# The shared network's down product of two token groups as three products of rounded words, with the experts' down weights loaded in two halves

## The reference, cut to what matters

```python
logits = x @ router_weight.T                 # 32 experts, top 4 of them per token
g = einsum('th,ehf->etf', x, w_gate); u = einsum('th,ehf->etf', x, w_up)      # F = 96
out = einsum('te,etf,efh->th', combine, silu(g) * u, w_down)
shared = silu(x @ sw_gate) * (x @ sw_up) @ sw_down                            # FS = 512
out = out + sigmoid(x @ sgate_w) * shared
```

## Time and profile before

| | us |
|---|---|
| median of 3 runs | 502.21 |
| lowest, highest | 502.06, 503.6 |
| the profiled execution | 502.63 |
| its span, first to last instruction | 500.5 |
| PE busy | 492.3 (98%) |
| DVE busy | 363.7 (73%) |
| ACT busy | 287.1 (57%) |
| POOL busy | 272.1 (54%) |

### The profile page before, as it was taken

One profiled execution on the slowest core, in us unless ns is written; L12 is line 12 of the kernel. 1 busy time (PEld: TensorE's weight loads), 2 busy tenths in 40 slices (PEclk: granted clock), 3 DMA queues, 4 the chain that ended last, 5 costly groups with the idle time before them and its releaser, 6 DMA issues.

```text
span 500.5 us, 13284 instructions
## 1 busy us (share of the span) xinstructions
PE 492.3 (98%) x3945; PEld 432.7 (86%) x3945; DVE 363.7 (73%) x1199; ACT 287.1 (57%) x719; POOL 272.1 (54%) x344
## 2 busy tenths in 40 slices
PE   7999999999999999999999999999999999999997
PEld 6999999999998888788888888888888888878886
DVE  5557888999886748834566777677767767379997
ACT  5777777877776635226477766677776662210110
POOL 2000477777777788881066767676676767500000
PEclk9999999999999999999999999999999999999999
DMA  6475577767745237934367666586766652399986
GB/s 212 136 224 184 172 255 222 220 222 214 219 165 179 101 110 181 250 132 108 91 186 229 202 197 195 174 238 182 217 197 194 183 188 101 96 402 377 327 361 208
DMA packets 65956, 100.77 MB, mean 201 GB/s; under 512 B 9856, under 2 KB 52864, under 8 KB 65792
## 3 DMA queue, kind: packets, MB, share of 16 engines
q1 hardware_dynamic: 48704, 60.30, 41.2%
q0 software_dynamic: 12672, 35.41, 19.5%
q10 hardware_dynamic: 4512, 4.23, 2.6%
HBM read 55.92 MB, written 43.97 MB: 200 GB/s over the span
## 4 chain that ended last, share of the span: by engine, by line
PE 90%; DVE 4%; DMA 2%; issue 1%; POOL 1%; ACT 1%; POOLq 0%; DVEq 0%; ACTq 0%; SPq 0%
PE bank L812 32%; PE bank L1108 14%; PE bank L1137 9%; PE bank L856 7%; PE bank L1104 5%; PE bank L1055 5%; PE bank L987 3%; PE bank L1018 3%; PE bank L1133 3%; PE bank L1004 3%; PE bank L1119 2%; PE bank L869 1%; PE bank L846 1%; POOL returned L515 1%; PE bank L972 1%
## 5 line engine op out<-in xcount | busy, mean ns | idle before, releaser
L484 POOL DMA_INDIRECT sent<-rows,slot x128 | 132.3, 1033 | 84.9 <-issue 83.6
L515 POOL DMA_INDIRECT returned<-arena,back x136 | 130.8, 962 | 77.1 <-DVE back L1638 35.6
L1108 PE MATMUL bank<-w_gu,arena 128*128 x416 | 79.7, 335 | 0.3 <-DVE resid L1278 0.3
L1108 PEld LDWEIGHTS bank<-w_gu,arena 128*128 128x128 f32 x416 | 66.3, 189 | 0.5 <-issue 0.5
L1606 DVE TENSOR_SCALAR arena<-bank,back_to 128x256 f32<-128x256 f32 x136 | 59.0, 475 | 3.0 <-issue 1.5
L542 ACT ACTIVATE act_t<-bank 128x512 f32<-128x512 f32 x24 | 14.4, 599 | 75.4 <-PE bank L812 75.4
L712 ACT COPY hnt<-w_gu 128x384 f32 x128 | 55.7, 511 | 0.0
L739 ACT ACTIVATE arena<-bank 128x192 f32<-128x192 f32 x68 | 22.4, 330 | 56.9 <-PE bank L1137 28.7
L1589 DVE TENSOR_TENSOR arena<-bank,arena 128x192 f32<-128x192 f32 x68 | 24.2, 356 | 41.6 <-ACT arena L739 40.2
L812 PE MATMUL bank<-w_hi_all,att_split 128*128 128x256 f32 x256 | 48.6, 292 | 0.0
L812 PE MATMUL bank<-hnt_rounded,ws_hi 128*128 128x512 f32 x160 | 48.4, 396 | 0.0
(11 more groups left out here) (216 smaller groups left out, 1057.3 us busy)
## 6 DMA issues: line engine op xcount, KB each, us to landing
arena<-returned SPq DMA_DIRECT2D x16, 1024.0 KB, 6.5
loaded<-sent SPq DMA_DIRECT2D x104, 134.0 KB
w_gu<-w_gate_up SPq DMA_DIRECT2D x32, 192.0 KB
sent<-rows SPq DMA_DIRECT2D x4, 1072.0 KB, 6.2
loaded<-sent SPq DMA_DIRECT2D x128, 33.5 KB
resid<-x SPq DMA_DIRECT2D x16, 256.0 KB, 3.7
att_plain<-ctx_t SPq DMA_DIRECT2D x16, 256.0 KB, 3.8
out<-resid ACTq DMA_DIRECT2D x7, 512.0 KB, 4.6
```

The lines of the kernel that those rows point to most:

```text
L484: pool.indirect_dma_start(out=sent, out_offset=bass.IndirectOffsetOnAxis(ap=slot[:, 2 * b + j, k:k + 1], axis=0), in_=rows[:, u, j, :], in ...
L515: pool.indirect_dma_start(out=returned, out_offset=bass.IndirectOffsetOnAxis(ap=back[:, t:t + 1], axis=0), in_=down_e[u][:, s, :], in_offs ...
L1108: last = pe.matmul(view[:, s, :], rows_t[:, s, c, :], w_gu[:, c, bass.ds(e[s], 1), :] .rearrange("p e f -> p (e f)"), start=(c == 0), stop ...
```

## The change

Four edits belong together.

1. The down products of groups 2 and 3 are made by `split_down`: `ws_d` and `act_t` are split into rounded words and rests, and 48 matmuls of float32r take the place of the 32 of float32. The order within a block f is: for each tile t hi by hi and hi by lo, then for each t lo by hi.
2. ACT rounds `ws_d` (`wd_hi`, 128x1024) behind group 2's first silu, and each block of `act_t` (`act_hi`, 128x512). DVE subtracts: `wd_lo` once (128x1024), ahead of group 2's third multiplication, and `act_lo` for each block (128x512), in the place of `act_t`.
3. `wd_hi`, `wd_lo` and `act_hi` lie in words 4096 to 8191 of `arena`, where the down weights of experts 16 to 31 come to lie. So SP loads only experts 0 to 15 where it loaded all, and the other 1.5 MB ahead of the tiles of pair 6, when `shared_psum` is 4.
4. TensorE's wait for `down_w` moves from ahead of step 0 to step 3, just ahead of the first `expert_down`, and waits for both loads; `copy_down` on ACT and DVE waits for both too.

```diff
@@ space @@
+        wd_hi, wd_lo = (plain_r[:, 4096 + FB * D * n:4096 + FB * D * (n + 1)].rearrange("p (f d) -> p f d", f=FB)
+                        for n in range(2))
+        act_hi = split[:, 0:FB * 512].rearrange("p (f t) -> p f t", f=FB)
         (w_plain,) = under(("w_plain", 4 * 512, F32))
+        (act_rounded,) = under(("act_rounded", FB * 512, F32R))
+        act_lo = act_rounded[:, :].rearrange("p (f t) -> p f t", f=FB)
         act_t = sb("act_t", [P, FB, 512])
...
+        def split_until(g, f):
+            return FB * (g - 2) + f + 1
@@ SP @@
-            sp.dma_start(w_dn, w_down).then_inc(S["down_w"], 16)
+            half = EXPERTS // 2
+            sp.dma_start(w_dn[:, 0:half, :], w_down[:, 0:half, :]).then_inc(S["down_w"], 16)
...
+                if pair == RING:
+                    wait(sp, "shared_psum", EARLY)
+                    sp.dma_start(w_dn[:, half:EXPERTS, :], w_down[:, half:EXPERTS, :]).then_inc(S["down_w"], 16)
                 wait(sp, "turned_psum", pair - RING + 1)
@@ ACT @@
+            def split_act_hi(g, f):
+                wait(act, "shared_act", FB * g + f + 1)
+                wait(act, "shared_psum", g if g > 2 else 0)
+                act.copy(act_hi[:, f, :], act_t[:, f, :]).then_inc(S["act_hi_ready"], 1)
+
             for g in range(2, EARLY):
                 for f in range(FB):
                     shared_silu(g, f)
+                    if g == 2 and f == 0:
+                        act.copy(wd_hi, ws_d[:, :, :]).then_inc(S["wd_hi_ready"], 1)
+                    if f > 0:
+                        split_act_hi(g, f - 1)
...
+                split_act_hi(g, FB - 1)
                 split_hn_hi(g + 1)
...
             def copy_down(pair, first):
                 if pair == FIRST_MIXED:
-                    act.wait_ge(S["down_w"], 16)
+                    act.wait_ge(S["down_w"], 32)
@@ PE @@
+            def split_down(g, behind={}):
+                wait(pe, "shared_added", GT * g)
+                if g == 2:
+                    pe.wait_ge(S["wd_lo_ready"], 1)
+                for f in range(FB):
+                    views = [sum_banks[t // 2][:, 256 * (t % 2):256 * (t % 2) + 256] for t in range(GT)]
+                    wait(pe, "act_hi_ready", split_until(g, f))
+                    for t in range(GT):
+                        pe.matmul(views[t], act_hi[:, f, P * t:P * t + P], wd_hi[:, f, :],
+                                  start=(f == 0 and t % 2 == 0), stop=False)
+                        pe.matmul(views[t], act_hi[:, f, P * t:P * t + P], wd_lo[:, f, :], start=False, stop=False)
+                    wait(pe, "act_lo_ready", split_until(g, f))
+                    for t in range(GT):
+                        last = pe.matmul(views[t], act_lo[:, f, P * t:P * t + P], wd_hi[:, f, :],
+                                         start=False, stop=(f == FB - 1 and t % 2 == 1))
+                    if f == FB - 1:
+                        last.then_inc(S["shared_psum"], 1)
+                    if f in behind:
+                        behind[f]()
...
-                shared_down(g, {2: first_transposes} if g == EARLY - 1 else {})
+                split_down(g, {2: first_transposes} if g == EARLY - 1 else {})
...
-            pe.wait_ge(S["down_w"], 16)
...
+                if pair == 3:
+                    pe.wait_ge(S["down_w"], 32)
                 if pair > 2:
                     expert_down(pair - 3, e[pair - 3])
@@ DVE @@
+            def split_act_lo(g, f):
+                wait(dve, "act_hi_ready", split_until(g, f))
+                dve.tensor_tensor(act_lo[:, f, :], act_t[:, f, :], act_hi[:, f, :].bitcast(F32), ALU.subtract) \
+                    .then_inc(S["act_lo_ready"], 1)
+
+            dve.wait_ge(S["wd_hi_ready"], 1)
+            dve.tensor_tensor(wd_lo, ws_d[:, :, :], wd_hi.bitcast(F32), ALU.subtract) \
+                .then_inc(S["wd_lo_ready"], 1)
             for g in range(2, EARLY):
                 for f in range(2 if g == 2 else 0, FB):
                     shared_mul(g, f)
+                    if g == 2 and f == 2:
+                        split_act_lo(g, 0)
+                    if f > 0:
+                        split_act_lo(g, f - 1)
+                split_act_lo(g, FB - 1)
                 split_hn_lo(g + 1)
...
             def copy_down(pair, first):
                 if pair == FIRST_MIXED:
-                    dve.wait_ge(S["down_w"], 16)
+                    dve.wait_ge(S["down_w"], 32)
```

More of the change, by code:

```diff
@@ L245, in build_xattn_moe @@
             "meant_ready", "meant_both_ready", "back_to_ready", "back_ready",
+            "wd_hi_ready", "wd_lo_ready", "act_hi_ready", "act_lo_ready",
             "sg_psum", "su_psum", "silu_ready", "shared_act", "shared_psum", "unit_psum", "shared_added",
```

## The result

The median of four runs is 511.5 us (510.13 to 511.7), against 502.24 us (502.06 to 503.6, four runs) for the kernel before on the same chip: a ratio of 1.0161, 95% interval 1.014 to 1.0182. The profiled execution took 510.13 us, with a span of 508.4 us against 500.5.

What follows compares the result with a forecast made beforehand. PE was taken as the bound, busy 98% of the span. Late weights 5.8, tiles 0.1 and clock 1.4 gave +7.3 us on 502.63, or 509.5 on the median, given as 509.2; range 504.8 to 511.8 us.

Steps and rivals of the forecast that it cites:

- the likeliest case: Second half lands late, PE idles 5.4 us before the first expert down product, clock falls; 509.2 us, chance 0.55.
- rival 4: Longer stall: sends held up 1.5 to 2 us, 10.8 us load, clock at half speed; 511.5 to 513 us, chance 0.15.
- the sum: Whole kernel: 5.8 us late weights, 0.1 tiles, 1.4 clock, +7.3 us on the profiled execution's 502.63.
- signs of being wrong: No PE idle time ahead of the first expert down product, or load issued before 242 us, would make the argument wrong.
- part 3: POOL's sends beside DVE's new subtractions: 0.7 us later (bounds 0 and 2), moving SP's whole list by as much.
- part 1 and 2: Down products of groups 2 and 3: matmuls gain 2.1 us, group 2's split waits leave 1.3 to 1.4 us.
- part 4: Second half of down weights: issued 243.0, 9.8 us to landing, PE waits 5.4 us; +5.8 us at first down product.
- rival 1: Second half lands sooner, at 248.6; PE waits about 2 us, clock stays; 503.7 to 505.7 us, chance 0.22.
- part 5: PE's clock after its idle wait: falls to 1.2 GHz, costing 1.4 us (bounds 0 and 2.7).
- the step: Load time of the second half: 1.57 MB at 213 GB/s, 7.4 us, plus 2.4 for start and end.
- Rivals 2 and 3: Weights in time, 1.4 us gained, 500.8 us (chance 0.04); or landing near 247 to 248.6, no change within 0.3% (0.04).
- Rival 5: Matmuls gain more or less than 1.4 us; lost at PE's wait, changes nothing while weights are late; no chance given.

Runs made afterwards that it cites:

- e1c: Changed kernel with the old float32 products and no splits, down weights still loaded in two halves: 510.43 us, ratio 1.0125 to the kernel before.
- e4c: Changed kernel with the wait for the second half of down weights moved from step 3 to step 8 on PE: 510.18 us, ratio 1.0126.
- e3c: Changed kernel with 24 unused matmuls ahead of PE's wait for the down weights: 509.39 us, ratio 1.0105 to the kernel before.
- e5: Changed kernel with the second half's load issued by ACT after group 3's down product, not by SP: 509.04 us, ratio 1.0113.
- e7c: Changed kernel with all down weights loaded at once as before, rounded words in attention's free spaces: 503.24 us, ratio 1.0004 to the kernel before.

## Why the prediction was right

The direction and the mechanism of the likeliest case held: the second half lands late, PE has one idle time of 5 to 6 us for it where there was none, and then works at the lower clock. The median lies 2.3 us above the forecast of 509.2, inside the whole range (504.8 to 511.8), but 0.5 us above that case's own range (507 to 511) and at the lower edge of rival 4. On the profiled execution the sum was 502.63 + 7.3 = 509.9, and 510.13 was measured. That this is so near is in part luck. PE's lateness at the first down product and behind it was forecast as 5.9 us, and is 4.9: the load was issued 1.7 us sooner, counted from the first load, and took 0.8 us longer. The clock was forecast as 1.4 us, and is 3.2. The earlier start of the whole profile then takes off 0.5 us.

One of the signs of being wrong did come: the load was issued at 240.83 us, before 242, and the last send ended 0.8 us earlier in place of up to 1 us later. The argument doesn't fall with it. In e1c and e4c the load was issued at 242.3 and 242.6 us, and PE waits as long, 5.5 and 5.7 us. The sign left no room for how much the sends vary (part 3 below).

**The products (part 1 and 2).** Gain 1.3 to 1.4 us at the end of group 3, by the two waits that stay in group 2. Measured: group 3 ends 1.4 us earlier from the common point. The subtraction for `wd_lo` on DVE, and what PE does at the start of group 2's down product:

```profile
211.22 1.16 DVE L1627 TENSOR_TENSOR att_rounded<-ws_d,att_rounded 128x1024 fp32r<-128x1024 f32 x1
```

```profile
212.49 0.36 PE L897 MATMUL bank<-att_rounded,att_split 128*128 128x256 f32 x1 [0.39 <-issue]
...
213.39 0.28 PE L899 MATMUL bank<-att_rounded,att_split 128*128 128x256 f32 x1
213.76 0.74 PE L902 MATMUL bank<-att_rounded,act_rounded 128*128 128x256 f32 x4
```

PE waits 0.39 us for `wd_lo` (forecast 0.4). From 213.39 to 213.76 are 0.37 us, where one product follows another in 0.12: some 0.25 us of wait for `act_lo` (forecast 0.3). The products themselves come every 0.12 us, as put down.

**The sends (part 3).** Forecast +0.7 us, measured -0.8 in the profiled execution. The mechanism is there, and smaller: in the stretch of the new subtractions two sends are long (timelines of POOL and DVE),

```profile
213.83 1.32 POOL L498 DMA_INDIRECT sent<-rows,slot  x1 [0.16 <-issue]
...
216.91 1.70 POOL L498 DMA_INDIRECT sent<-rows,slot  x1 [0.16 <-issue]
...
213.02 1.28 DVE L1623 TENSOR_TENSOR act_rounded<-act_t,att_split 128x512 fp32r<-128x512 f32 x2
...
216.54 1.22 DVE L1289 TENSOR_TENSOR hnt_rounded<-hnt,hn_hi 128x1024 fp32r<-128x1024 f32 x1 [0.26 <-ACT hn_hi L581]
```

where one of 1.61 was the earlier trace rows, which adds 0.4 us. The one of 1.70 stands beside the old subtraction (L1289, L1244 before), so that the new ones lengthen a single send, by 0.35 us. Both long sends start while a subtraction runs and end about one normal duration after it. A send that a subtraction joins later isn't lengthened: the one at 215.54 takes 0.97 us, though a subtraction starts 0.05 us behind it. What I hadn't seen is that the sends of attention, where the kernels are the same, differ from one trace to the next by more than that. Their time over 0.96 us a send, summed until 192 us, is 7.9 us in before, 7.7 in e1c, e3c and e4c, and 6.6 in after, e5 and e7c: two levels, some 1.1 us apart. In before this costs next to nothing, as POOL has 1% of the chain. Since the change hangs SP's load, and PE on it, on the last send, it now reaches the end. It fits that the other three runs of the kernel after took 511.4 to 511.7 us, 1.3 to 1.6 us more than the profiled one; that they are the executions with the slower sends is argued, not shown. Against these three the sum was 1.6 us low.

**The load (part 4).** Issue forecast for 243.0, measured 240.83: 1.5 us of it by the sends, 0.5 by the earlier start. Duration forecast 9.8 us with bounds of 6.3 and 10.8, measured 10.56 with tile loads in the same queue (9.2 for the first half, without them). By the DMA queue's records the last packet of 16 KB moves at 249.0 to 249.3 us, 8.4 us after the issue, where the step had 7.4, and the load counts as landed only 2.2 us behind it, while tile loads already fill the DMA engines (the step had 2.4 for start and end). So the step's rate was near, and rival 1, by which the half lands in 6.3 us, is refuted by every run: no half took less than 9.2. The estimate worked out from the Trainium skill ("SBUF — State Buffer", the section on the DMA setup-cost knee) was 5.6 us for the half; the measurement decides against it. Wait forecast 5.4 us, measured 5.9. The wait of 1.7 us for pair 4's tiles, which I had ahead of it, isn't in the profiled execution, where SP came earlier, but it is there in e3c (1.5) and e4c (1.7), where SP issued the load 49.8 and 50.0 us after the first one (forecast 50.1, measured in after 48.5). It changes nothing, since PE only loses there what it would lose later.

**The clock (part 5).** Forecast 1.4 us, between 0 and 2.7; measured 3.2, above the bound. e3c shows that it is the idling's doing, and gives 2.5 of it back. This is the term that was sized worst: I took the fall from the earlier trace rows as coming within 2.7 us of the last product and had no row for the return. The clock fell later than that, 5.3 us after the last product, and was still low for 6.2 us after the restart, at half speed, which is 3.1 us. The bound was too narrow because no row of before shows a restart after an idle time.

**Rivals 2 and 3** needed the half in 3.4 to 5 us: refuted. **Rival 4** came half true, with the clock at half speed for several us and a load near 10.8, but with the sends on the other side. **Rival 5** (the products' gain is lost at the wait) is what the trace of after shows, and e1c agrees with it.

## What to carry to other kernels

A transfer that is off the critical path because it is issued 50 us early can become the path when a change of memory layout lets it start only late; before a buffer is reused under it, work out from the trace when the issuing queue will get to it, at what rate it moved before, and who is queued behind it. Splitting a large load helps only if the small transfers that the next steps need don't have to run beside it: here it held them up from both queues that were tried. And an idle time on PE has a second price, the low clock after the restart, which can be more than half of the first.

## What was not expected of the hardware

- After an idle time of 5.9 us PE worked for 6.2 us at 1.2 GHz, at a cost of 3.2 us. In the three other kernels with such an idle time the clock fell sooner after the last product (2.7 us in e1c, 2.3 in e4c, 2.9 in e5) and came back sooner after the restart (4.0, 3.5, 3.3 us), so that a longer idle time isn't the only thing that sets the cost. With products running through the wait it didn't fall at all.
- A load with rows of 16 KB in each of 96 partitions held up tile loads behind it in its own queue (10.2 us to landing instead of at most 2.6) and in another one (8.4 us, with nothing moved in that queue from 238 to 243 us). Whether the size of the rows is the reason, no run here shows.
- In the kernel after, this load counts as landed only 2.2 us after its last packet of 16 KB moved.
- A send of POOL that starts while a DVE subtraction of two SBUF operands runs is lengthened (0.97 us to 1.3 to 1.7). The time of attention's sends lies at two levels, some 1.1 us apart, in traces of kernels that are the same up to there; what sets the level is open.
